# Token convolution stage: all eight chunks in one unrolled sequence, and expert loads split 24 and 40

## The chip, the cores and the metric

The kernel runs on one core of one Trainium2 chip. The metric is the device time of one execution in microseconds (us). The engines named below are TensorE (PE; its weight loads are listed apart, as PEld), VectorE (DVE), ScalarE (ACT), GpSimd (POOL) and SyncE (SP); the last issues most of the DMAs, POOL the gathers.

## What is computed

A small language-model tower over 16 x 256 tokens of 64 features, nine stages one after the other. The change is in the first stage, and it moves work across the border to the second.

```python
def _L0_tok_ref(x, emb, W, b):           # first stage
    offsets = jnp.arange(-(KSIZE // 2), KSIZE // 2 + 1)        # KSIZE = 9
    idx = jnp.clip(x[..., None] + offsets, 0, INP_SIZE - 1)
    gathered = emb[idx]                                        # 9 neighbouring rows of the table
    out = jnp.einsum('btkh,ohk->bto', gathered, W) + b
    return out
...
h = _L0_tok_ref(...)
h = h + _L0_attn_ref(_layernorm(h), ...)  # second stage, linear attention
h = h + _L0_ffn_ref(_layernorm(h), ...)   # third stage: each run of 64 tokens has one of 16 experts
...
```

## The kernel before, in words

Tokens are cut into `CHUNKS` = 8 chunks of 512; a chunk is four groups of 128 tokens. `W` = 4 chunks are in work at a time, each with a PSUM tensor `PS[w]` of its own, two banks wide; `ITERS` = 2 rounds of four chunks cover all. `H` holds the tower's running result.

In `token_convolution` each chunk goes through this chain. POOL issues four indirect DMAs (L226), each of which fetches for 128 tokens the nine neighbouring table rows, 2304 bytes in one piece. The buffer `win` has six slots, so chunk 6 has to wait until PE has read chunk 0 (`windows_read`), chunk 7 until chunk 1. PE transposes the first half of the windows into `PS[w]` (eight transposes, L246, r = 0; called r0 in the prediction); DVE and ACT copy one bank each to `winT` (L302, L283); PE transposes the second half (r1), and they copy again (L305, L286). PE transposes the tails, the ninth row (L256, L257), and ACT copies them (L289). PE convolves: eight matmuls (L264), each shown twice, and one for the tails (L267). ACT copies the result (L292), PE transposes it back (L274), and DVE adds the bias into `H` (L310).

The order on PE is by steps over a whole round: r0 of all four chunks, r1 of all four, tails of all four, convolution of all four, turning back of all four; then the second round, which first waits until all four chunks of the first are in `H`. PE's program is written out; ACT's is a hardware loop of two rounds. In the last round DVE also prepares the layer norm of the second stage (`prepare_next`): statistics and, after POOL's power, the normalised values of chunks 0 to 3. A block ends when every engine has reached its end.

SP issues the weights, and then in `Experts.load` (L513 to L515) one load of 129 KB for each run of 64 tokens, 64 in all: it reads the expert's number from `route`, and issues the DMA from a hardware loop. 32 loads (chunks 0 to 3) stand in the first stage's block and 32 in that of `linear_attention`. They are needed by the third stage, `routed_ffn`, whose POOL program begins with a wait for all of them.

Of the kernel before, what the change touches and what calls it, by code (L numbers as in the profile page):

```python
# [17 lines left out]
ALU = mybir.AluOpType  # L18
# [81 lines left out]

class NormBuffers:


# [64 lines left out]
def prepare_next(nc, v, H, C, stats, apply):  # L170

    N, x_of = C.next_norm, lambda w: groups(chunk_of(H, 0, w))
    N.prepared = True
    if stats:
        norm_stats(nc, v, N.S, x_of, N, 0)
    if apply and N.centre_only:
        norm_centre(nc, v, N.S, x_of, N, N.xc)
    elif apply:
        norm_apply(nc, v, N.S, x_of, N, N.xc, N.xn, 0)
# [11 lines left out]
def token_convolution(nc, H, PS, C, dram):  # L191
    with ExitStack() as ctx:
        S = semaphores(nc, "tok",
                        "ids windows_read winT_low winT_high winT_ps0 winT_ps1 winT2_low winT2_high "
                        "tailT yT_ps yT y_ps h_new")
        sb = lambda name, shape, dt=F32: ctx.enter_context(nc.sbuf_tensor(name, shape, dt))
        ids = sb("tok_ids", [P, CHUNKS * G4], I32)
        slots = W + 2
        slot = lambda it, w: it * W + w if w < slots - W else w - it * (slots - W)
        win = sb("tok_windows", [P, slots, G4, KS * D])  # L200
        winT = sb("tok_windowsT", [P, W, KC, G4 * P])
        tailT = sb("tok_tailsT", [P, W, U * P])
        yT = sb("tok_yT", [P, W, U * P])
        block = ctx.enter_context(nc.Block())
        gathered = [nc.alloc_semaphore(f"tok_gathered{c}") for c in range(CHUNKS)]
        w_main = C["tok_w"][:, 0:KC * D].rearrange("p (k f) -> p k f", f=D)
        w_tail = C["tok_w"][:, KC * D:]

        @block.sync
        def _(sp):  # L210
            sp.dma_start(ids[:], dram["ids"]).then_inc(S["ids"], 16)
            C.experts.load_route(sp)
            C.load(sp, "early")
            C.load(sp, "gate")
            C.experts.load(sp, range(CHUNKS // 2))

        @block.gpsimd
        def _(pool):
            pool.wait_ge(S["ids"], 16)
            for it in range(ITERS):  # L220
                for w in range(W):
                    if it * W + w >= slots:
                        pool.wait_ge(S["windows_read"], it * W + w - slots + 1)
                    for g in range(G4):
                        at = (it * W + w) * G4 + g
                        nc.gpsimd.indirect_dma_start(  # L226
                            win[:, (it * W + w) % slots, g, :], None, dram["emb"],
                            bass.IndirectOffsetOnAxis(ap=ids[:, at:at + 1], axis=0)).then_inc(gathered[it * W + w], 16)
            prepare_next_rstd(nc, pool, C)

        @block.tensor
        def _(pe):
            ident = C["ident"]
            pe.wait_ge(C.sem("base"), C.count("base"))
            for it in range(ITERS):
                for r in range(KC // 2):
                    for w in range(W):
                        if r == 0:
                            pe.wait_ge(gathered[it * W + w], 16 * G4)
                        else:  # L240
                            pe.wait_ge(S["winT_low"], it * W + w + 1)
                            pe.wait_ge(S["winT_high"], it * W + w + 1)
                        for k in range(2):
                            for g in range(G4):
                                at = (2 * r + k) * P
                                ins = nc.tensor.transpose(PS[w][:, k, g * P:(g + 1) * P], win[:, slot(it, w), g, at:at + P],  # L246
                                                          ident)
                        ins.then_inc(S["winT_ps0"] if r == 0 else S["winT_ps1"], 1)
                for w in range(W):
                    pe.wait_ge(C.sem("base"), C.count("base"))  # L250
                    pe.wait_ge(S["winT2_low"], it * W + w + 1)
                    pe.wait_ge(S["winT2_high"], it * W + w + 1)
                    for u in range(U):

                        tails = PS[w][:, 0, u * P:(u + 1) * P]
                        nc.tensor.transpose(tails, win[:, slot(it, w), 2 * u + 1, KC * P - D:], ident)  # L256
                        ins = nc.tensor.transpose(tails[0:D], win[:, slot(it, w), 2 * u, KC * P:], ident)  # L257
                    ins.then_inc(S["windows_read"], 1)
                for w in range(W):
                    odd_even = lambda ap: ap.rearrange("p (u h q) -> p h u q", u=U, h=2)  # L260
                    y = [PS[w][h * D:(h + 1) * D, 1, 0:U * P] for h in range(2)]
                    for k in range(KC):
                        for h in range(2):
                            nc.tensor.matmul(y[h], w_main[:, k, :], odd_even(winT[:, w, k, :])[:, h], start=(k == 0),  # L264
                                             stop=False)
                    pe.wait_ge(S["tailT"], it * W + w + 1)
                    nc.tensor.matmul(PS[w][:, 1, 0:U * P], w_tail, tailT[:, w], start=False, stop=True)\  # L267
                        .then_inc(S["yT_ps"], 1)
                for w in range(W):
                    pe.wait_ge(C.sem("base"), C.count("base"))  # L270
                    pe.wait_ge(S["yT"], it * W + w + 1)
                    for u in range(U):
                        at = slice(u * P, (u + 1) * P)
                        ins = nc.tensor.transpose(PS[w][:, 0, at], yT[:, w, at], ident)  # L274
                    ins.then_inc(S["y_ps"], 1)
                pe.wait_ge(S["h_new"], it * W + W)

        @block.scalar
        def _(act):
            with act.Fori(0, ITERS) as it:  # L280
                for w in range(W):
                    act.wait_ge(S["winT_ps0"], it * W + w + 1)
                    nc.scalar.copy(winT[:, w, 1, :], PS[w][:, 1, :]).then_inc(S["winT_high"], 1)  # L283
                for w in range(W):
                    act.wait_ge(S["winT_ps1"], it * W + w + 1)
                    nc.scalar.copy(winT[:, w, 3, :], PS[w][:, 1, :]).then_inc(S["winT2_high"], 1)  # L286
                for w in range(W):
                    act.wait_ge(S["windows_read"], it * W + w + 1)
                    nc.scalar.copy(tailT[:, w], PS[w][:, 0, 0:U * P]).then_inc(S["tailT"], 1)  # L289
                for w in range(W):  # L290
                    act.wait_ge(S["yT_ps"], it * W + w + 1)
                    nc.scalar.copy(yT[:, w, :], PS[w][:, 1, 0:U * P]).then_inc(S["yT"], 1)  # L292
                act.wait_ge(S["y_ps"], it * W + W)

        @block.vector
        def _(v):
            v.wait_ge(C.sem("base"), C.count("base"))

            def one_round(it, last):
                for w in range(W):  # L300
                    v.wait_ge(S["winT_ps0"], it * W + w + 1)
                    nc.vector.tensor_copy(winT[:, w, 0, :], PS[w][:, 0, :]).then_inc(S["winT_low"], 1)  # L302
                for w in range(W):
                    v.wait_ge(S["winT_ps1"], it * W + w + 1)
                    nc.vector.tensor_copy(winT[:, w, 2, :], PS[w][:, 0, :]).then_inc(S["winT2_low"], 1)  # L305
                if last:
                    prepare_next(nc, v, H, C, True, True)
                for w in range(W):
                    v.wait_ge(S["y_ps"], it * W + w + 1)
                    nc.vector.tensor_tensor(groups(chunk_of(H, it, w)), groups(PS[w][:, 0, 0:CW]),  # L310
                                            bcast(C["tok_b"], 1, G4), ALU.add).then_inc(S["h_new"], 1)
                v.wait_ge(S["h_new"], it * W + W)

            with v.Fori(0, ITERS - 1) as it:
                one_round(it, False)
            one_round(ITERS - 1, True)

# [3 lines left out]
def linear_attention(nc, H, PS, C, dram):  # L323
    with ExitStack() as ctx:
# [16 lines left out]

        @block.sync
        def _(sp):
            C.experts.load(sp, range(CHUNKS // 2, CHUNKS))

        @block.gpsimd
        def _(pool):
# [2226 lines left out]
```

## Time and profile before

| | us |
|---|---|
| median of three runs (lowest to highest) | 947.04 (946.51 to 947.96) |
| the profiled execution | 946.42 |
| its span, first to last instruction | 944.6 |
| first stage: last addition into `H` ends | 80.5 |
| second stage: its block ends | about 148.6 |
| mean granted TensorE clock | 0.865 |

All times of a row are counted from the first instruction of the span. The page's own summary:

```profile
span 944.6 us, 13089 instructions
PE 703.9 (75%) x4437; PEld 447.7 (47%) x4437; DVE 560.0 (59%) x1472; ACT 337.7 (36%) x612; POOL 200.0 (21%) x170
DMA  8552221000000100000000000005001000000001
```

A digit of the last line is the mean busy share, in tenths, of the core's 16 DMA engines in one fortieth of the span (23.6 us). A row of the timeline gives start, duration, engine, line, operation and what it writes and reads, then in brackets how long the engine was idle before and who released it. The engine name SPq is SP's own instruction stream.

### The profile page before, as it was taken

Reading aid. Unit: us, or ns where it says so; the run is one execution under the profiler, and the core shown is the slowest. Engines: PE = TensorE matmul, PEld = TensorE weight load, DVE = VectorE, ACT = ScalarE, POOL = GpSimd, SP = SyncE. Lnnn points to the kernel's source line nnn. Section 1 sums busy time; section 2 is a strip of 40 time slices with the busy share of each in tenths; the row PEclk is TensorE's granted clock in tenths of the full one; section 3 lists DMA queues with packets and bytes.
Section 4 is the critical chain, followed back from the end, with each engine's and each line's share of the span. In section 5 each row is a group of like instructions: output and inputs, shape, how many; then the busy total and the mean of one; then the engine's idle time right before and its main releaser. Section 6 shows DMA issues by size and latency. Waiting matters only on the chain. (4 is left out here: it accounts for less than half of the span.)

```text
span 944.6 us, 13089 instructions
## 1 busy us (share of the span) xinstructions
PE 703.9 (75%) x4437; PEld 447.7 (47%) x4437; DVE 560.0 (59%) x1472; ACT 337.7 (36%) x612; POOL 200.0 (21%) x170
## 2 busy tenths in 40 slices
PE   2587667978882699987489856877785978999674
PEld 1465555647661323224365435543221645887363
DVE  0144883444547557756685278645556899444597
ACT  1132112425451345434123312412333958333253
POOL 6421110130201010113520133110204557000320
PEclk9799787988996599997679977995978989899887
DMA  8552221000000100000000000005001000000001
GB/s 281 175 154 74 79 63 59 2 1 1 1 1 0 60 1 1 1 29 1 1 1 1 1 1 1 1 22 231 1 0 32 1 0 0 1 1 2 1 14 32
DMA packets 17708, 31.38 MB, mean 33 GB/s; under 512 B 6226, under 2 KB 14450, under 8 KB 16882
## 3 DMA queue, kind: packets, MB, share of 16 engines
q1 hardware_dynamic: 15090, 21.18, 7.1%
q0 software_dynamic: 2560, 9.44, 3.2%
q8 instruction: 35, 0.57, 0.3%
q14 instruction: 23, 0.19, 0.1%
HBM read 29.54 MB, written 1.05 MB: 32 GB/s over the span
## 5 line engine op out<-in xcount | busy, mean ns | idle before, releaser
L150 POOL TENSOR_TENSOR norm_rstd<-norm_var,minus_half 128x16 f32<-128x16 f32 x16 | 47.5, 2967 | 398.3 <-DVE norm_var L144 398.3
L1184 ACT ACTIVATE m_g<-PS,w_slot 128x512 f32<-128x512 f32 x96 | 60.8, 686 | 70.6 <-PE PS L1237 64.3
L1137 DVE TENSOR_TENSOR m_gw<-m_g,PS 128x512 f32<-128x512 f32 x96 | 61.4, 683 | 39.2 <-PE PS L1245 26.7
L1237 PE MATMUL PS<-m_xT,w_slot 64*128 64x512 f32 x192 | 70.9, 696 | 7.0 <-ACT m_g L1184 6.8
L1261 PE MATMUL PS<-m_gw,w_slot 128*64 128x512 f32 x192 | 56.4, 657 | 0.0
L1392 POOL TENSOR_TENSOR win_rms<-win_ms,win_minus_half 128x24 f32<-128x24 f32 x8 | 33.3, 4164 | 89.3 <-DVE win_ms L1438 89.3
L246 PE MATMUL PS<-w_base,tok_windows 128*128 128x128 f32 x128 | 21.1, 337 | 29.4 <-DMA tok_windows<-in_emb,tok_ids 21.2
L1531 DVE TENSOR_TENSOR win_out<-PS,w_slot 128x512 f32<-128x512 f32 x32 | 20.6, 686 | 33.0 <-PE PS L1702 33.0
L1245 PE MATMUL PS<-m_gT,m_sel 48*128 48x512 bf16 x96 | 24.3, 423 | 15.8 <-DVE m_gw L1137 10.0
L1968 ACT COPY rat_xf<-PS 64x512 f32 x32 | 33.7, 1053 | 5.4 <-PE PS L2024 5.2
L1700 PE MATMUL PS<-win_big,win_v 128*128 128x512 f32 x64 | 32.2, 627 | 4.4 <-ACT win_big L1604 4.2
L226 POOL DMA_INDIRECT tok_windows<-in_emb,tok_ids x32 | 30.6, 957 | 21.9 <-PE PS L257 9.5
L2044 PE MATMUL PS<-w_slot,rat_ht 128*128 128x256 f32 x128 | 34.7, 396 | 0.0
L132 DVE BATCH_NORM_STATS2 norm_halves<-H 128x6 f32<-128x64 f32 x256 | 33.9, 216 | 0.9 <-PEq L2550 0.9
L1594 ACT ACTIVATE win_terms<-win_terms 128x768 f32<-128x768 f32 x8 | 6.8, 845 | 75.9 <-DVE win_terms L1494 75.9
L246 PEld LDWEIGHTS PS<-w_base,tok_windows 128*128 128x128 f32 x128 | 19.0, 177 | 31.0 <-issue 13.1
L1237 PEld LDWEIGHTS PS<-m_xT,w_slot 64*128 64x128 f32 x192 | 24.2, 217 | 18.2 <-ACT m_g L1184 14.9
L2024 PE MATMUL PS<-w_slot 128*128 128x512 f32 x64 | 31.6, 618 | 0.0
L1657 PE MATMUL PS<-w_base,win_big 128*128 128x128 f32 x64 | 12.9, 368 | 22.8 <-DVE win_big L1469 22.8
L1245 PEld LDWEIGHTS PS<-m_gT,m_sel 48*128 48x128 bf16 x96 | 5.5, 94 | 50.1 <-DVE m_gw L1137 30.3
L1914 DVE COPY rat_hf<-PS 128x512 f32 x16 | 16.6, 1040 | 20.7 <-PE PS L2044 20.7
L302 DVE COPY tok_windowsT<-PS 128x512 f32<-128x512 f32 x8 | 5.4, 690 | 38.4 <-issue 19.9
(331 smaller groups left out, 1715.2 us busy)
## 6 DMA issues: line engine op xcount, KB each, us to landing
rff_routed<-in_routed SPq DMA_DIRECT2D x64, 129.0 KB, 2.0
rat_hf<-in_rat_den SPq DMA_DIRECT2D x1, 2048.0 KB, 7.7
rat_hf<-in_rat_num SPq DMA_DIRECT2D x1, 2048.0 KB, 12.2
w_slot<-in_w_rat SPq DMA_DIRECT2D x1, 1716.5 KB, 15.8
w_slot<-in_w_win SPq DMA_DIRECT2D x1, 1379.5 KB, 5.9
w_slot<-in_w_m SPq DMA_DIRECT2D x1, 1329.0 KB, 6.0
w_slot<-in_w_early SPq DMA_DIRECT2D x1, 1156.0 KB
out<-H SPq DMA_DIRECT2D x8, 128.0 KB, 2.2
```

The costliest lines, as they stand in the source:

```text
L132: ins = nc.vector.bn_stats(N.st[:, w * G4 + g, :], x_of(w)[:, g, :])
L150: nc.gpsimd.tensor_tensor(N.rstd[:], N.var[:], C.minus_half[:], ALU.pow).then_inc(S["norm_rstd"], 1)
L246: ins = nc.tensor.transpose(PS[w][:, k, g * P:(g + 1) * P], win[:, slot(it, w), g, at:at + P], ident)
L1137: nc.vector.tensor_tensor(gw[:, i % 2, half, :], g[:, i % 2, half, :], gate_bank[half], ALU.mult)\
L1184: nc.scalar.activation(g[:, i % 2, half, :], hid_bank[(n - 1) % 3], ACT.Gelu, bias=b1[:, s:s + 1])\
L1237: nc.tensor.matmul(hid_bank[n % 3], w1[lane(half), s, :], pair_of(xT, pair)[lane(half)], start=True, stop=True).then_inc(S["hid_ps"], 1)
L1261: ins = nc.tensor.matmul(y[half], w2[:, s, :], gw[:, i % 2, half, :], start=False, stop=(s == SL - 1))
L1392: nc.gpsimd.tensor_tensor(rms[:, w].rearrange("p u j h -> p (u j h)"), ms[:, w].rearrange("p u j h -> p (u j h)"), minus_half[:], ALU.pow)\
L1700: ins = nc.tensor.matmul(PS[w][:, u, :], v[:, w, u, half, :], probT[w][:, half * U + u, :], start=True, stop=(u == 0))
L1968: ins = nc.scalar.copy(dst, banks[4 + s % 4][rows, :].rearrange("p (t x l) -> p t x l", t=2, x=2))
L2024: ins = nc.tensor.matmul(banks[4 + s % 4], xd[:, w, 2 * u + half].rearrange("p a f -> p (a f)"), dft[:, u, :], start=(u == 0), stop=(u == ...
L2044: ins = nc.tensor.matmul(bank[:, 2 * LT:], part_of[c], odd[:, c, :], start=(c == 0), stop=(c == 1))
```

## The change

`ladder` is new. It puts each chunk's stages at fixed steps: stage k of chunk c comes at step `spacing * c + k`, with spacing 2, so a chunk enters every two steps and a chunk's own stages (r0, r1, tails, convolution, turning back) follow in consecutive steps. PE, ACT and DVE all follow it, written out for all eight chunks; the hardware loops of ACT and DVE in this stage are gone. PE's waits for the end of a round are replaced by a wait for the chunk that used the same `PS[w]` last. DVE's norm statistics are placed at step 11 and the application at step 14. The buffers keep their sizes, and no operation of a chunk is added or removed. In a step the order on PE is: turn back, convolve, tails, r1, r0. SP's 64 expert loads are cut after chunk 2: 24 in the first block, 40 in the second.

```diff
+def ladder(stages, depth, spacing, then=None):
+
+    for n in range(spacing * (CHUNKS - 1) + depth):
+        for k, stage in stages:
+            if n >= k and (n - k) % spacing == 0 and (n - k) // spacing < CHUNKS:
+                stage((n - k) // spacing)
+        if then:
+            then(n)
...
+        spacing, depth = 2, 5
...
-            C.experts.load(sp, range(CHUNKS // 2))
+            C.experts.load(sp, range(3))
...
-            for it in range(ITERS):
-                for r in range(KC // 2):
-                    for w in range(W):
-                        if r == 0:
-                            pe.wait_ge(gathered[it * W + w], 16 * G4)
...
-                pe.wait_ge(S["h_new"], it * W + W)
+            def turn_windows(c, r):
+                w = c % W
+                if r == 0:
+                    pe.wait_ge(gathered[c], 16 * G4)
+                    if c >= W:
+                        pe.wait_ge(S["h_new"], c - W + 1)
+                else:
+                    pe.wait_ge(S["winT_low"], c + 1)
+                    pe.wait_ge(S["winT_high"], c + 1)
...
+            def turn_tails(c):
+                w = c % W
+                pe.wait_ge(S["winT2_low"], c + 1)
...
+            def convolve(c):
+                w = c % W
+                pe.wait_ge(S["winT2_high"], c + 1)
...
+            ladder([(4, turn_y), (3, convolve), (2, turn_tails), (1, lambda c: turn_windows(c, 1)),
+                    (0, lambda c: turn_windows(c, 0))], depth, spacing)
...
-            with act.Fori(0, ITERS) as it:
...
+            ladder([(3, copy_y), (2, copy_tails), (1, lambda c: copy_windows(c, 1)), (0, lambda c: copy_windows(c, 0))],
+                   depth, spacing)
...
+            def then(n):
+                if n == spacing * 3 + 5:
+                    v.wait_ge(S["h_new"], W)
+                    prepare_next(nc, v, H, C, True, False)
+                if n == spacing * 3 + 8:
+                    prepare_next(nc, v, H, C, False, True)
+
+            ladder([(4, add_bias), (1, lambda c: copy_windows(c, 1)), (0, lambda c: copy_windows(c, 0))], depth, spacing,
+                   then)
+            v.wait_ge(S["h_new"], CHUNKS)
...
-            C.experts.load(sp, range(CHUNKS // 2, CHUNKS))
+            C.experts.load(sp, range(3, CHUNKS))
```

## Rows read from the trace of the kernel before

**Rows 1.** Busy time by stretch; columns are named in the first line.

```profile
core 0: us, PE busy (x) PEld busy (x) DVE busy (x) ACT busy (x) POOL busy (x), PEclk, DMA share, GB/s
...
20.50:38.00 17.50, 6.30 (x32) 5.67 (x32) 0.69 (x1) 0.59 (x1) 10.44 (x11) 0.88 0.75 231
38.00:43.60 5.60, 4.77 (x23) 4.65 (x24) 3.87 (x6) 3.43 (x7) 0.00 (x0) 0.50 0.26 71
...
47.40:55.50 8.10, 5.90 (x37) 3.04 (x36) 0.00 (x0) 0.58 (x2) 4.74 (x5) 1.00 0.90 283
...
59.80:81.00 21.20, 19.94 (x160) 15.01 (x160) 12.68 (x44) 8.50 (x17) 3.06 (x1) 1.00 0.31 82
```

**Rows 2.** Timeline, first gather burst: PE's transposes and DVE's copies that follow them.

```profile
13.10 1.94 PE L246 MATMUL PS<-w_base,tok_windows 128*128 128x128 f32 x8 [13.10 <-DMA tok_windows<-in_emb,tok_ids]
...
15.07 0.69 DVE L302 COPY tok_windowsT<-PS 128x512 f32<-128x512 f32 x1 [15.07 <-issue]
...
17.73 1.97 PE L246 MATMUL PS<-w_base,tok_windows 128*128 128x128 f32 x8 [2.69 <-DMA tok_windows<-in_emb,tok_ids]
...
20.54 0.69 DVE L302 COPY tok_windowsT<-PS 128x512 f32<-128x512 f32 x1 [4.78 <-issue]
...
22.05 1.97 PE L246 MATMUL PS<-w_base,tok_windows 128*128 128x128 f32 x8 [2.36 <-DMA tok_windows<-in_emb,tok_ids]
...
27.12 4.33 PE L246 MATMUL PS<-w_base,tok_windows 128*128 128x128 f32 x24 [3.10 <-DMA tok_windows<-in_emb,tok_ids]
...
38.08 1.29 DVE L302 COPY tok_windowsT<-PS 128x512 f32<-128x512 f32 x2 [16.85 <-remote]
...
38.83 3.67 PE L246 MATMUL PS<-w_base,tok_windows 128*128 128x128 f32 x16 [7.38 <-DVE tok_windowsT L302]
```

**Rows 3.** Timeline, second gather burst: PE's last convolution matmul and ACT's copy behind it.

```profile
46.79 0.70 PE L267 MATMUL PS<-tok_tailsT,w_base 128*128 128x256 f32 x2
...
49.30 0.70 PE L267 MATMUL PS<-tok_tailsT,w_base 128*128 128x256 f32 x2
...
50.88 0.37 ACT L292 COPY tok_yT<-PS 128x256 f32<-128x256 f32 x1 [5.49 <-PE PS L267]
...
55.30 0.74 ACT L292 COPY tok_yT<-PS 128x256 f32<-128x256 f32 x2 [4.04 <-remote]
```

**Rows 4.** Line L226, POOL's gathers, in 4 to 35 us and in 43 to 54 us.

```profile
L226 POOL DMA_INDIRECT tok_windows<-in_emb,tok_ids x24: 945/949/1197, 4.1 to 33.2; - x24
...
L226 POOL DMA_INDIRECT tok_windows<-in_emb,tok_ids x8: 947/949/949, 43.6 to 52.4; - x8
```

**Rows 5.** SP's expert loads (L515) by stretch, SP's timeline, its waits.

```profile
L515 SPq DMA_DIRECT2D rff_routed<-in_routed x9: 13/351/716, 4.8 to 35.2; - x9
...
22.61 13.32 SPq L515 DMA_DIRECT2D rff_routed<-in_routed  x2
...
L515 SPq DMA_DIRECT2D rff_routed<-in_routed x12: 347/349/351, 60.8 to 78.2; - x12
...
SPq L192 <- PEq L192: 2.2, 1, 2.2
```

**Rows 6.** Timeline of the second round, when all windows have landed.

```profile
59.86 7.21 PE L246 MATMUL PS<-w_base,tok_windows 128*128 128x128 f32 x64 [0.77 <-DVE H L310]
...
60.99 0.59 ACT L283 COPY tok_windowsT<-PS 128x512 f32<-128x512 f32 x1 [0.28 <-PE PS L246]
...
68.74 1.95 PE L264 MATMUL PS<-tok_windowsT,w_base 128*64 128x256 f32 x16
70.62 0.70 PE L267 MATMUL PS<-tok_tailsT,w_base 128*128 128x256 f32 x2
71.25 1.95 PE L264 MATMUL PS<-tok_windowsT,w_base 128*64 128x256 f32 x16
...
78.68 1.13 PE L274 MATMUL PS<-w_base,tok_yT 128*128 128x128 f32 x8
79.09 1.42 DVE L310 TENSOR_TENSOR H<-PS,w_base 128x256 f32<-128x256 f32 x4 [3.59 <-PE PS L274]
```

**Rows 7.** SP in the second stage: its loads, and its wait at the block's end.

```profile
L515 SPq DMA_DIRECT2D rff_routed<-in_routed x32: 342/350/356, 82.6 to 133.8; - x32
...
SPq L324 <- PEq L324: 14.3, 1, 14.3
```

More of the change, by code:

```diff
@@ L198, in token_convolution @@
         slots = W + 2
-        slot = lambda it, w: it * W + w if w < slots - W else w - it * (slots - W)
+        spacing, depth = 2, 5
         win = sb("tok_windows", [P, slots, G4, KS * D])
@@ L219, in _ @@
             pool.wait_ge(S["ids"], 16)
-            for it in range(ITERS):
-                for w in range(W):
[L222 to L228, printed above, removed]
+            for c in range(CHUNKS):
+                if c >= slots:
+                    pool.wait_ge(S["windows_read"], c - slots + 1)
+                for g in range(G4):
+                    at = c * G4 + g
+                    nc.gpsimd.indirect_dma_start(
+                        win[:, c % slots, g, :], None, dram["emb"],
+                        bass.IndirectOffsetOnAxis(ap=ids[:, at:at + 1], axis=0)).then_inc(gathered[c], 16)
             prepare_next_rstd(nc, pool, C)
@@ L234, in _ @@
             pe.wait_ge(C.sem("base"), C.count("base"))
-            for it in range(ITERS):
-                for r in range(KC // 2):
-                    for w in range(W):
-                        if r == 0:
-                            pe.wait_ge(gathered[it * W + w], 16 * G4)
[L240 to L275, printed above, removed]
-                pe.wait_ge(S["h_new"], it * W + W)
@@ new lines, in turn_windows @@
+            def turn_windows(c, r):
[7 more added lines that the diff above has]
+                    pe.wait_ge(S["winT_high"], c + 1)
+                for k in range(2):
+                    for g in range(G4):
+                        at = (2 * r + k) * P
+                        ins = nc.tensor.transpose(PS[w][:, k, g * P:(g + 1) * P], win[:, c % slots, g, at:at + P], ident)
+                ins.then_inc(S["winT_ps0"] if r == 0 else S["winT_ps1"], 1)
@@ new lines, in turn_tails @@
+            def turn_tails(c):
+                w = c % W
+                pe.wait_ge(S["winT2_low"], c + 1)
+                for u in range(U):
+                    tails = PS[w][:, 0, u * P:(u + 1) * P]
+                    nc.tensor.transpose(tails, win[:, c % slots, 2 * u + 1, KC * P - D:], ident)
+                    ins = nc.tensor.transpose(tails[0:D], win[:, c % slots, 2 * u, KC * P:], ident)
+                ins.then_inc(S["windows_read"], 1)
+            def convolve(c):
+                w = c % W
+                pe.wait_ge(S["winT2_high"], c + 1)
+                odd_even = lambda ap: ap.rearrange("p (u h q) -> p h u q", u=U, h=2)
+                y = [PS[w][h * D:(h + 1) * D, 1, 0:U * P] for h in range(2)]
+                for k in range(KC):
+                    for h in range(2):
+                        nc.tensor.matmul(y[h], w_main[:, k, :], odd_even(winT[:, w, k, :])[:, h], start=(k == 0),
+                                         stop=False)
+                pe.wait_ge(S["tailT"], c + 1)
+                nc.tensor.matmul(PS[w][:, 1, 0:U * P], w_tail, tailT[:, w], start=False, stop=True).then_inc(S["yT_ps"], 1)
@@ L278, in _, with turn_y @@
+            def turn_y(c):
+                w = c % W
+                pe.wait_ge(S["yT"], c + 1)
+                for u in range(U):
+                    at = slice(u * P, (u + 1) * P)
+                    ins = nc.tensor.transpose(PS[w][:, 0, at], yT[:, w, at], ident)
+                ins.then_inc(S["y_ps"], 1)
+            ladder([(4, turn_y), (3, convolve), (2, turn_tails), (1, lambda c: turn_windows(c, 1)),
+                    (0, lambda c: turn_windows(c, 0))], depth, spacing)
         @block.scalar
@@ L279, in _, with copy_windows @@
         def _(act):
-            with act.Fori(0, ITERS) as it:
[L281 to L293, printed above, removed]
+            def copy_windows(c, r):
+                w = c % W
+                act.wait_ge(S["winT_ps1"] if r else S["winT_ps0"], c + 1)
+                nc.scalar.copy(winT[:, w, 2 * r + 1, :], PS[w][:, 1, :]).then_inc(S["winT2_high"] if r else S["winT_high"], 1)
@@ new lines, in copy_tails, with copy_y @@
+            def copy_tails(c):
+                act.wait_ge(S["windows_read"], c + 1)
+                nc.scalar.copy(tailT[:, c % W], PS[c % W][:, 0, 0:U * P]).then_inc(S["tailT"], 1)
+            def copy_y(c):
+                act.wait_ge(S["yT_ps"], c + 1)
+                nc.scalar.copy(yT[:, c % W, :], PS[c % W][:, 1, 0:U * P]).then_inc(S["yT"], 1)
+            ladder([(3, copy_y), (2, copy_tails), (1, lambda c: copy_windows(c, 1)), (0, lambda c: copy_windows(c, 0))],
+                   depth, spacing)
@@ L297, in _, with copy_windows, add_bias @@
             v.wait_ge(C.sem("base"), C.count("base"))
[L299 to L316, printed above, removed]
+            def copy_windows(c, r):
+                w = c % W
+                v.wait_ge(S["winT_ps1"] if r else S["winT_ps0"], c + 1)
+                nc.vector.tensor_copy(winT[:, w, 2 * r, :], PS[w][:, 0, :]).then_inc(S["winT2_low"] if r else S["winT_low"], 1)
+            def add_bias(c):
+                v.wait_ge(S["y_ps"], c + 1)
+                nc.vector.tensor_tensor(groups(H[:, c * CW:(c + 1) * CW]), groups(PS[c % W][:, 0, 0:CW]),
+                                        bcast(C["tok_b"], 1, G4), ALU.add).then_inc(S["h_new"], 1)
+            def then(n):
[7 more added lines that the diff above has]
+            v.wait_ge(S["h_new"], CHUNKS)
 def linear_attention(nc, H, PS, C, dram):
```

## The prediction

> **What bounds the kernel now.** Only the first stage changes its order, so I read the table of stretches over it first, then the timeline of PE with the copies that answer it, then the gathers, and SP last. The stage has three candidates for its end: the arrival of the windows, PE's own work, and SP's expert loads.
>
> The windows come in two bursts. 24 gathers are issued from 4.1 to 33.2 us, one every 1.25 us; then POOL waits for a free slot, and eight more go from 43.6 to 52.4 [rows 4]. PE's work can be read where nothing holds it, in the second round: 64 transposes in 7.2 us, so 0.9 for a block of eight; the tails fill the gap up to 68.7, 0.45 a chunk; a convolution takes 2.5 from start to start; turning back 1.1 for four, 0.28 a chunk [rows 6]. That is 5.0 us a chunk, 40 us for eight, at the full clock. PE is 94% busy there (19.94 of 21.2) [rows 1].
>
> The first round is quite different. In 20.5 to 38 PE is busy for 6.3 of 17.5 us, and DVE and ACT do one copy each [rows 1]. PE finishes chunk 0's block at 15.04 and the copy starts at 15.07. Chunk 1's ends at 19.70, its copy starts 0.8 us late, at 20.54. Chunk 2's ends at 24.02, and its copy starts at 38.08, 14 us late, though DVE had nothing else to do [rows 2]. In the second burst the same thing: a convolution that ends at 47.5 is answered at 50.88, one that ends at 50.0 at 55.30 [rows 3]. So while gathers run, PE's signals arrive late, and the delay ends about when the windows of the burst have landed. I call this the freeze. It is the main fact for this change, since the new order has more such handshakes inside the bursts. The name "remote" of the releaser says that the profile does not show what released it.
>
> SP suffers as well: nine loads in the first 35 us, with over 12 us between the eighth (22.6) and the ninth. Undisturbed it needs (78.2 - 60.8) / 11 = 1.58 us a load. It was done only 2.2 us before the block's end [rows 5]; with 32 loads in the block the end could come hardly 2 us earlier, whatever PE does. So PE and SP are both nearly on the path now.
>
> **The change part by part.** First the windows. POOL's wait for chunk 6 hangs on the tails of chunk 0, now PE's third block instead of its ninth. If the signal comes through, gathers run without a pause: 4.1 + 32 x 1.25 = 44.2, and with the 3.0 us that chunk 3 took from its last issue (24.1) to PE's start (27.12) the last windows are there at 47.2 instead of about 56 [rows 2, 4].
>
> PE if handshakes pass. r0 of chunk 0 ends at 15.0, the copy at 15.8; r1 in the slow form (1.97 for eight) ends 17.8, copy 18.6, tails 0.9 to 19.5, r0 of chunk 1 to 21.4, convolution 0 at double price to 26.4 [rows 2, 6]. The double price is the nearest row: eight transposes take 1.94 to 1.97 there against 0.9 later, and 38 to 43.6 shows the same with a granted clock of 0.50, the 1.2 GHz level, after PE had idled [rows 1, 2]. With PE now nearly always busy I take the full level afterwards. r1 of chunk 1, turning back chunk 0, tails 1 and r0 of chunk 2 end at 29.4. From here each chunk costs 5.0 plus one wait that the old order hid: the tails of a chunk come right behind its r1, and need DVE's copy of 0.69 and some 0.1 for two signals, of which the turning back of the chunk before fills 0.28; 0.5 left. Five more chunks at 5.5 bring r0 of chunk 7 to 56.9, ten us behind its windows, so arrival is no longer the bound. Then convolution 6 2.5, r1 0.9, copy 0.8, tails 0.45, convolution 7 2.7, copy 0.45, back 0.3, addition 0.4: 65.4, against 80.5 now.
>
> DVE's statistics and normalisation move to steps 11 and 14. They take about 3 us each between PE's signals; behind them on DVE stand the copies of chunks 6 and 7. Between the copies of r0 and the demand of r1 lies a convolution of 2.5, so I price this at nothing, with 1 us as its bound if that cover fails. POOL's power stands behind the last gather, which is issued by 44 to 50, long before step 11. The end-of-round waits that vanish are worth about 1 us (the gap before 59.86), contained in the sum.
>
> The loops. ACT's first copy after its loop edge waits 0.28 us for PE, no more than any other [rows 6]; unrolling is worth 0 here. By the Trainium skill ("Runtime: NRT & Kernel Launch", Instruction fetch mechanics) a taken branch outside the fetched window costs a fetch from memory and full unrolling avoids it; no wait of this stage's rows is at the branch, and by that rule the sum would gain at most the 0.28.
>
> SP. 24 loads in place of 32. From 60.8 on the pace is 1.58, so the 24th is issued at 60.8 + 3 x 1.58 = 65.5 under today's pause in the gathers, and SP is done 0.6 later, 66.1. If gathers run on to 47, the slow pace lasts longer: ninth at 35.2, the tenth one slow interval (12.6) later at 47.8, then 14 x 1.58 = 22.1, so 69.9 and done at 70.5 [rows 5]. These are the two ends; I take 70.5, since unbroken gathers are what the PE sum assumed. SP then ends the block, 5 us behind PE.
>
> The second block gets 40 loads. 31 intervals took 51.2 us, 1.65 each (a stretch of them is slower); SP waited 14.3 at the end. Eight more take 13.2, so 1.1 us of slack remain [rows 7]. Priced at 0, bound 1 us; the third stage's wait for the last landing gets no later than its start.
>
> The sum: the first block ends at 70.5 instead of 81.0 (78.8 + 2.2), a gain of about 10.4. The profiled execution gives 946.4 - 10.4 = 936.0; the median of the runs lies 0.6 above the profiled one, so 936.6, rounded to **937**.
>
> **The rivals.** *Freeze (slower).* Chunk 1's r0 ends at 21.4, where signals are between 0.8 us late (19.7) and 14 us late (24.0). If it is caught, nothing follows in the new order: r1 of chunk 1 needs its copy, and PE has only convolution 0 to do, where the old order still had r0 of chunks 2 and 3 and two r1 blocks. Chunk 0's tails (19.5) would just come through, chunk 6's gathers run on to 39.2, and the freeze to their landing at 42. PE has then done 5.6 of its 40 us; left are 34.3, six waits of 0.5, 2.5 for the slow clock after idling (5 us at half speed), 3 us for a second freeze by chunk 7's gathers (the old one left PE about that idle before 55.5), 1 for the end: 85.8, that is 5.3 later than now, **952**. It decides if a signal given between 20 and 24 us waits for the landing. For it: six of six handshakes deep in a burst did. Against it: the delays grow with the work PE had queued behind the gathers (40 transposes ran unanswered from 22 to 31.5 us; two convolutions in the second burst), and the new order queues little: the handshakes with a short queue before them, at 15 and 20 us, passed with the DMA engines as busy.
>
> *SP is not held.* By the Trainium skill ("DMA: Bandwidth & Descriptors", Queues, rings and completion order) each DMA engine alternates between the queues that have work, packet by packet. That rule alone would let expert loads pass beside gathers; the trace's interval of 12.6 us speaks against it. As a mechanism in rows: 24 loads at 1.58 end by 43, and PE sets the end at 65.4, a gain of 15: **932**.
>
> *Half frozen.* Some handshakes pass late, PE loses 10 to 14 of the 15 us, and the time stays at 945 to 949.
>
> *The second block overruns or the norm falls on the path.* 1 to 5 us given back: 938 to 942.
>
> **How the numbers follow.** Forecast 0.36 (about 934 to 939), SP not held 0.14, second block or norm 0.06, half frozen 0.10, freeze 0.34. Within 0.2% (945.1 to 948.9, about what a measurement of this kernel can tell from no change) lies the half-frozen case: same 0.10, faster 0.36 + 0.14 + 0.06 = 0.56, slower 0.34. Both signs hold much, so the range goes from 931 to 953; the forecast's own is 933 to 940.
>
> **What would show it.** Right: gathers issued without a pause from 4 to 44 us; copies within 1 us of PE's blocks all through; PE above 85% busy from 27 to 62; SP's block wait near zero with its last load at 66 to 70; the second stage's length unchanged at 67.6. The freeze would show as DVE and ACT idle for over 10 us after a PE block, releaser "remote", and as a first block that ends after 81. Wrong in any case if SP's pace outside bursts is not 1.58, or PE drops to 0.50 in the middle of the ladder.

## The result and the profile after

The changed kernel takes 958.69 us (957.58 to 960.18, four runs) against 946.77 (945.58 to 947.96, four runs): a ratio of 1.0129, interval 1.0111 to 1.0147. The forecast of 937 lies on the wrong side, and above all the time lies beyond the range. The profiled execution has 957.58 us, its span is 955.8, 11.2 more than before. Block by block, read from the ends of the blocks on SP (the same barriers in both traces), this is where it went:

| block | before | after | difference |
|---|---|---|---|
| first stage ends at | 81.0 | 88.3 | +7.3 |
| linear attention | 67.6 | 68.0 | +0.4 |
| routed_ffn | 56.6 | 57.1 | +0.4 |
| batchnorm_attention | 101.1 | 98.5 | -2.7 |
| gelu_moe_128 and window_attention | 327.7 | 327.9 | +0.3 |
| gelu_moe_64 | 90.4 | 93.1 | +2.7 |
| rational_convolution | 158.2 | 158.5 | +0.4 |
| depth_ffn, the last | 61.3 | 63.7 | +2.4 |

(Differences are taken before rounding.) Two thirds of the loss are in the changed stage, the rest in stages whose code is the same, but for the eight loads that moved into the second. First the stretches of the changed kernel, which answer [rows 1]:

```profile
core 0: us, PE busy (x) PEld busy (x) DVE busy (x) ACT busy (x) POOL busy (x), PEclk, DMA share, GB/s
...
20.50:38.00 17.50, 6.09 (x30) 4.04 (x30) 0.40 (x1) 0.67 (x2) 13.23 (x15) 0.83 0.83 252
38.00:47.00 9.00, 2.58 (x11) 2.18 (x12) 1.62 (x3) 1.45 (x3) 0.93 (x1) 0.50 0.38 116
47.00:60.00 13.00, 11.36 (x80) 8.41 (x79) 2.81 (x6) 3.56 (x8) 3.78 (x4) 0.92 0.57 167
```

PE is busy for 6.1 us of 17.5 in the gathers, and then 2.6 of 9.0; the old order had work for the second stretch as well (4.8 of 5.6 in 38 to 43.6). The timeline, which answers [rows 2]:

```profile
15.57 1.97 PE L257 MATMUL PS<-w_base,tok_windows 128*128 128x128 f32 x8 [0.86 <-ACT tok_windowsT L298]
...
20.21 0.69 DVE L318 COPY tok_windowsT<-PS 128x512 f32<-128x512 f32 x1 [4.69 <-remote]
...
21.87 1.92 PE L257 MATMUL PS<-w_base,tok_windows 128*128 128x128 f32 x8
23.71 2.64 PE L277 MATMUL PS<-tok_windowsT,w_base 128*64 128x256 f32 x16
...
27.20 0.37 ACT L302 COPY tok_tailsT<-PS 128x256 f32<-128x256 f32 x1 [6.41 <-remote]
...
43.32 0.69 DVE L318 COPY tok_windowsT<-PS 128x512 f32<-128x512 f32 x1 [22.41 <-remote]
43.80 0.38 ACT L306 COPY tok_yT<-PS 128x256 f32<-128x256 f32 x1
44.06 1.97 PE L257 MATMUL PS<-w_base,tok_windows 128*128 128x128 f32 x8 [15.74 <-DVE tok_windowsT L318]
```

r1 of chunk 0 ends at 17.5 and is answered 2.7 us late; the tails end at 22.1 (the fourth starts at 21.65 and takes 0.42) and are answered at 27.2; r0 of chunk 1 ends at 23.8 and its copy starts at 43.32, 19.5 us late. All that PE could do meanwhile was convolution 0, answered at 43.80. Then PE stands for 15.74 us. This is the rival "freeze", except that the rival had let the tails come through in time. The gathers answer [rows 4], SP's waits [rows 5]:

```profile
L235 POOL DMA_INDIRECT tok_windows<-in_emb,tok_ids x28: 942/946/1197, 4.0 to 38.0; - x28
...
48.20 0.94 POOL L235 DMA_INDIRECT tok_windows<-in_emb,tok_ids  x1 [9.27 <-PE PS L267]
```

```profile
SPq L202 <- PEq L202: 21.1, 1, 21.1
SPq L342 <- PEq L342: 2.0, 1, 2.0
```

Chunk 6's gathers did run on, chunk 7's waited for PE until 48.2. SP was done 21 us before the block's end, so it held nothing here; in the second block, with 40 loads, it was done 2.0 us before the end. The free-running part of the ladder shows its price per chunk:

```profile
58.61 1.04 PE L257 MATMUL PS<-w_base,tok_windows 128*128 128x128 f32 x8
...
64.31 1.04 PE L257 MATMUL PS<-w_base,tok_windows 128*128 128x128 f32 x8
...
66.13 0.33 PE L266 MATMUL PS<-w_base,tok_windows 128*128 128x128 f32 x1 [0.57 <-DVE tok_windowsT L318]
...
87.45 0.42 DVE L322 TENSOR_TENSOR H<-PS,w_base 128x256 f32<-128x256 f32 x1 [3.82 <-PE PS L287]
```

5.70 us a chunk (64.31 - 58.61), with the wait of 0.57 before the tails, against the 5.0 of [rows 6].

### The profile page after: what moved, and what is told of

Same layout as the page of the kernel before. It is cut to its first block and busy times, and to the rows that moved or that the text cites. A ratio compares the mean times of both kernels' runs of the same rounds, so it can differ in the third digit from the quotient of the medians.

```text
span 955.8 us, 13059 instructions
## 1 busy us (share of the span) xinstructions
PE 706.2 (74%) x4437; PEld 447.2 (47%) x4437; DVE 560.0 (59%) x1472; ACT 336.3 (35%) x611; POOL 198.8 (21%) x170
## 5 line engine op out<-in xcount | busy, mean ns | idle before, releaser
L1155 DVE TENSOR_TENSOR m_gw<-m_g,PS 128x512 f32<-128x512 f32 x96 | 61.4, 683 | 41.8 <-PE PS L1263 28.1
L1255 PE MATMUL PS<-m_xT,w_slot 64*128 64x512 f32 x192 | 70.5, 694 | 6.9 <-ACT m_g L1202 6.8
L318 DVE COPY tok_windowsT<-PS 128x512 f32<-128x512 f32 x16 | 11.1, 691 | 64.6 <-remote 27.1
L257 PE MATMUL PS<-w_base,tok_windows 128*128 128x128 f32 x128 | 20.9, 318 | 29.4 <-DVE tok_windowsT L318 15.7
```

Of the source, the lines that this page charges most:

```text
L1155: nc.vector.tensor_tensor(gw[:, i % 2, half, :], g[:, i % 2, half, :], gate_bank[half], ALU.mult)\
L1255: nc.tensor.matmul(hid_bank[n % 3], w1[lane(half), s, :], pair_of(xT, pair)[lane(half)], start=True, stop=True).then_inc(S["hid_ps"], 1)
```

## The experiments

Theory F: the loss comes from the freeze, that is from PE's blocks being answered late while gathers run, which the new order meets with too little work queued. Rivals: the split 24 and 40; the ladder as such; the bytes of the gathers; SP's loads beside them. Each group of runs was on another chip, which turned out to be the main finding. All runs in one table; "beside" is the unchanged kernel on the same chip, "block 1" the end of the first block in the profile:

| run | chip | us | beside | block 1 |
|---|---|---|---|---|
| the pair above: before / after | not named | 946.77 / 958.69 | | 81.0 / 88.3 |
| split_only | 3 | 936.61 | 937.11 | 69.5 |
| ladder_32 | 3 | 934.42 | 937.11 | 66.7 |
| narrow_ladder | 3 | 931.73 | 937.11 | 63.3 |
| narrow_rounds | 3 | 933.86 | 937.11 | 68.0 |
| after_again | 5 | 934.86 | 935.92 | 65.5 |
| before_again | 5 | 933.88 | 935.92 | 68.7 |
| spacing1 | 5 | 931.76 | 935.92 | 64.1 |
| paced | 5 | 935.59 | 935.92 | 66.0 |
| after_third | 15 | 936.13 | 938.79 | 66.1 |
| loads_late | 15 | 953.91 | 938.79 | 84.6 |
| narrow_third | 15 | 934.56 | 938.79 | 64.5 |
| spacing1_timed | 15 | 933.21 | 938.79 | 64.1 |
| narrow_fourth | 2 | 932.77 | 939.05 | 63.8 |
| spacing1_fourth | 2 | 931.55 | 939.05 | 63.9 |
| narrow_fifth | 9 | 933.01 | 938.89 | 64.1 |
| after_sixth | 7 | 935.91 | 934.09 | 66.5 |
| narrow_sixth | 7 | 933.79 | 934.09 | 64.3 |

split_only, after_again, ladder_32 and spacing1_timed have seven to ten runs; the others one. On chips 3, 5 and 15 the unchanged kernel ran 42 times, between 933.2 and 939.8.

### The two parts of the change alone

split_only is the kernel before with this edit:

```diff
-            C.experts.load(sp, range(CHUNKS // 2))
+            C.experts.load(sp, range(3))
...
-            C.experts.load(sp, range(CHUNKS // 2, CHUNKS))
+            C.experts.load(sp, range(3, CHUNKS))
```

> The kernel before, with only the expert loads cut 24 and 40. Theory (the freeze of PE's signals in the gather bursts, met by the new order, makes the whole loss): the first stage still ends at 80.5 to 81, since PE ends it, and the second grows by 0 to 1 us: ratio 1.000 to 1.001. Rival (the split costs, because 40 loads overrun the second stage): the second stage grows by 2 us or more, ratio 1.002 or above.

Measured: ratio 0.9986, interval 0.9971 to 1.0002. The split costs nothing that can be measured here. The block end of 81 was missed: it came at 69.5, with PE's copies all in time. (In the pair above, where the second block was done 2.0 us after SP, it cost nothing that shows either: that block is 0.4 longer.)

ladder_32 is the changed kernel with the loads cut 32 and 32 again:

```diff
-            C.experts.load(sp, range(3))
+            C.experts.load(sp, range(CHUNKS // 2))
...
-            C.experts.load(sp, range(3, CHUNKS))
+            C.experts.load(sp, range(CHUNKS // 2, CHUNKS))
```

> The changed kernel with 32 and 32 loads as before. Theory of the freeze: SP waited 21 us at the end of the changed first block, and 8 loads take 12.6 us, so the block still ends at 88; the ratio to the kernel before stays 1.012 to 1.013, at most 0.5 us better than the changed kernel. Rival (split costs): the ratio falls to 1.010 or lower.

Measured: ratio 0.9961, interval 0.9939 to 0.9983. The theory's expectation failed, and the rival's "1.010 or lower" is met by the number alone, since split_only shows no cost of the split: the ladder, 1.3% slower in the pair above, is 0.4% faster here, and its block ends 2.8 us before that of split_only on the same chip. SP had 12.7 us left in it. So neither the split nor the ladder makes the loss by itself; something else differs between the chips, or between the times of the measurements.

### The same two kernels on other chips

> The changed kernel, unaltered, on whatever chip it gets. Theory F (a freeze of PE's signals, which only some chips or states show, decides the sign): where the profile shows no copy later than 2 us behind PE's block, the first block ends at 66 to 68 and the ratio to the kernel before is 0.995 to 0.998; where it shows the freeze (copies over 10 us late between 20 and 43), the block ends at 86 to 90 and the ratio is 1.011 to 1.015. Rival (40 loads in the second stage cost more than the first stage gains): the ratio is 1.00 or more without any freeze.

> The kernel before, unaltered, for its profile beside the one of the changed kernel on the same chip. Theory F: without a freeze the first block ends at 69 to 71 and the time is 934 to 939; with it the block ends at 80 to 82 and the time is 945 to 948. The loads' pace tells the same: 1.5 to 1.6 us from the start without, one interval of over 10 us with the freeze.

Measured for the changed kernel, ten runs on chip 5: 934.86, ratio 0.9984, interval 0.9966 to 1.0002. The profiles of both on chip 5 show no freeze. The expectations were just missed (blocks at 65.5 and 68.7 instead of 66 to 68 and 69 to 71, the ratio a little above 0.998), and the interval does not quite exclude 1.00, the number of the rival that the second stage takes the gain; but that stage is only 1.0 us longer (68.6 against 67.6). The unchanged kernel there, to be laid beside [rows 1] and [rows 2]:

```profile
20.50:38.00 17.50, 12.13 (x82) 10.69 (x82) 4.22 (x7) 4.91 (x10) 12.96 (x14) 1.00 0.95 316
```

```profile
22.76 1.97 PE L246 MATMUL PS<-w_base,tok_windows 128*128 128x128 f32 x8 [2.92 <-DMA tok_windows<-in_emb,tok_ids]
...
24.77 0.69 DVE L302 COPY tok_windowsT<-PS 128x512 f32<-128x512 f32 x1 [4.20 <-PE PS L246]
27.84 6.29 PE L246 MATMUL PS<-w_base,tok_windows 128*128 128x128 f32 x40 [3.11 <-DMA tok_windows<-in_emb,tok_ids]
...
29.84 0.69 DVE L302 COPY tok_windowsT<-PS 128x512 f32<-128x512 f32 x1 [4.38 <-PE PS L246]
```

Chunk 2's transposes end at 24.73 and are answered at 24.77, where [rows 2] has 14 us. The releaser has a name again (PE, not "remote"). PE does 12.1 us of work in the stretch instead of 6.3. The DMA engines are busier than on the first chip, 0.95 and 316 GB/s against 0.75 and 231: the freeze is no matter of full DMA engines. Part of the difference in rate is that POOL issues 14 gathers in the stretch instead of 11; the other part is SP's loads, which keep their pace inside the bursts:

```profile
L515 SPq DMA_DIRECT2D rff_routed<-in_routed x28: 347/350/372, 4.8 to 47.1; - x28
...
DMA to landing us min/median/max: 2.0/4.2/4.4
```

28 loads in 42.3 us, 1.57 each, where [rows 5] has nine in 30.4 us. They land after 4.2 us, against the 2.1 of loads issued when no gathers run, but that holds nothing up. By the Trainium skill ("DMA: Bandwidth & Descriptors", Queues, rings and completion order) the engines alternate between the queues packet by packet. On this chip the trace agrees: loads at full pace beside gathers, each landing 2 us later. The first chip's trace does not speak against it, as the prediction held, since there SP issued few loads in the burst, and their landings are not recorded.

What slowed there was SP's own instruction stream. The instruction that sets up each load takes, least, median and longest in ns, in the changed kernel on the first chip and on chip 5:

```profile
L533 SPq MOVE rff_routed<-in_routed x24: 2/29/701, 4.6 to 66.6; - x24
...
L533 SPq MOVE rff_routed<-in_routed x24: 29/29/29, 4.8 to 40.8; - x24
```

PE's stream slowed too. In the second burst of the kernel before, on the first chip, a convolution that waits for no other engine falls apart into single matmuls 0.7 us apart:

```profile
52.28 0.45 PE L264 MATMUL PS<-tok_windowsT,w_base 128*64 128x256 f32 x2 [0.63 <-issue]
...
53.71 0.38 PE L264 MATMUL PS<-tok_windowsT,w_base 128*64 128x256 f32 x1 [0.97 <-issue]
...
54.43 0.48 PE L267 MATMUL PS<-tok_tailsT,w_base 128*128 128x256 f32 x1 [0.34 <-issue]
```

So the freeze is not only PE's signals arriving late; whether a late copy comes from a late signal or from a slow stream of the engine that waits, the rows do not tell.

The changed kernel on chip 5:

```profile
20.50:38.00 17.50, 15.80 (x117) 11.30 (x116) 5.14 (x9) 5.38 (x11) 13.24 (x14) 1.00 0.96 319
```

```profile
19.48 1.91 PE L257 MATMUL PS<-w_base,tok_windows 128*128 128x128 f32 x8
...
21.43 0.69 DVE L318 COPY tok_windowsT<-PS 128x512 f32<-128x512 f32 x1 [2.91 <-PE PS L257]
...
64.62 0.42 DVE L322 TENSOR_TENSOR H<-PS,w_base 128x256 f32<-128x256 f32 x1 [3.82 <-PE PS L287]
```

The forecast's PE sum comes out here at both ends: r0 of chunk 1 ends at 21.4 (21.4 forecast) and is answered at 21.43; the last addition ends at 65.04 (65.4 forecast). Between them two errors cancel:

```profile
23.86 0.70 PE L280 MATMUL PS<-tok_tailsT,w_base 128*128 128x256 f32 x2
...
26.71 1.04 PE L257 MATMUL PS<-w_base,tok_windows 128*128 128x128 f32 x8
...
55.32 1.04 PE L257 MATMUL PS<-w_base,tok_windows 128*128 128x128 f32 x8
```

Convolution 0 ends at 24.56 instead of 26.4, because the double price was right for its first part only, and r0 of chunk 2 ends at 27.75 instead of 29.4. The next five chunks then take 28.6 us instead of 27.5. The rival "SP is not held" is this case: the 24th load is issued at 40.8.

> The changed kernel, unaltered, on a further chip. Theory F (some chips show the freeze of PE's signals, others not): either the first block ends at 65 to 67 and the kernel before takes 934 to 939 beside it, or the block ends at 86 to 90 and the kernel before takes 945 to 948. Rival (the freeze was an accident of single executions): any other pairing of the two.

> The changed kernel, unaltered, on a further chip. Without the freeze: first block ends at 65 to 67, the kernel before takes 933 to 940. With it: 86 to 90, and 945 to 948 for the kernel before.

Both came out as "without": blocks at 66.1 and 66.5, and the unchanged kernel at 933 to 940. So there are seven chips, one with the freeze in both kernels and, by their times, in all eight of its runs, and six without it in seventeen profiles (on chip 9 only narrow gathers were profiled, and the kernel before speaks by its time, 938.89). The pair's chip was not met again, so whether it is the chip or a state in which it was then can't be told. No experiment ran under the freeze: what is said of it rests on the two profiles of the pair.

### What in the gathers could make it

narrow_ladder and narrow_rounds gather 1024 bytes a token instead of 2304, and PE reads the first 256 elements twice, and the tails from there too:

```diff
-                        win[:, c % slots, g, :], None, dram["emb"],
+                        win[:, c % slots, g, 0:2 * P], None, dram["emb"],
...
-                        at = (2 * r + k) * P
+                        at = k * P
...
```

> The changed kernel with gathers of 1024 bytes a token instead of 2304; PE transposes the first 256 elements twice and takes the tails from there too, so the convolution is computed on wrong windows, with the same number and shape of instructions on every engine. Theory A (the freeze comes from the bytes that the gathers move, the DMA engines being 0.75 to 0.9 busy): the DMA share falls below 0.5, the copies follow PE within 1 us, PE sets the end of the first stage at 64 to 68 us. Theory B (it comes from the act of gathering, POOL's descriptors, at one gather every 1.25 us as before): the freeze stays, the first stage ends at 84 or later. Theory C (the ladder is slow by itself): as A without a freeze, yet the end at 75 or later.

> The kernel before with the same narrow gathers of 1024 bytes. Theory A: no freeze; the first round is done at about 49, the second at about 70, but SP's 32 loads then set the end if they take 1.58 us each from the start (they would end at 56, so no); first stage ends at 68 to 72, later than in the ladder with narrow gathers by 2 to 6 us, so the change would have paid without the freeze. Theory B: freeze as before, end at 80.

Measured: blocks end at 63.3 and 68.0, so without a freeze the ladder is worth 4.7 us of the block with these gathers. Neither number proves anything for theory A, since this chip has no freeze with full gathers either; and the DMA share stayed at 0.71 in 20.5 to 38, where A expected less than 0.5.

> The changed kernel with gathers of 1024 bytes a token (wrong windows, same instructions), on the same chip as after_third. With a freeze there: gone if it comes from the bytes moved (block ends at 63 to 66), still there if from the act of gathering (84 or later). Without a freeze: the block ends 2 to 3 us before the changed kernel's, since the first windows land earlier, as on the first of these chips.

> The changed kernel with gathers of 1024 bytes a token (wrong windows, same instructions), on a further chip. If the kernel before takes 945 to 948 beside it, the chip shows the freeze, and then: gone from this kernel (block ends at 61 to 65) if it comes from the bytes moved, still there (84 or later) if from the act of gathering. If the kernel before takes 933 to 940, the chip shows none, and this kernel's block ends at 61 to 65.

> As narrow_fourth, on a further chip: if the kernel before takes 945 to 948 beside it the chip shows the freeze, and the first block of this kernel ends at 61 to 65 if the bytes moved make it, at 84 or later if the act of gathering does. If the kernel before takes 933 to 940 there is none, and the block ends at 61 to 65.

> As narrow_fifth, beside after_sixth on the same chip: with a freeze there, 61 to 65 if the bytes moved make it, 84 or later if the act of gathering does; without, 61 to 65.

64.5, 63.8, 64.1 and 64.3, each beside a kernel before of 934 to 940: no freeze on any of these chips, and the question of bytes against gathering stays open. (narrow_third is 1.6 us before after_third, where 2 to 3 were expected.)

loads_late holds SP's loads back:

```diff
+            sp.wait_ge(gathered[CHUNKS - 1], 16 * G4)
             C.experts.load(sp, range(3))
```

> The changed kernel with SP's 24 loads held back until the last windows have landed; so the bursts hold gathers alone, and SP's instruction stream is silent in them. With a freeze: if SP's traffic takes part in it, the copies follow PE within 2 us and gathers run to 44; if not, copies late by over 10 us as in the changed kernel. Without a freeze: loads end at 48 + 24 x 1.58 = 86, SP sets the end of the block at 86 to 87, the copies are as before.

Measured: the block ends at 84.6 (86 to 87 expected), and SP's wait for the last windows was 43.4 us. PE's work in the bursts is the same with and without loads beside the gathers:

```profile
20.50:38.00 17.50, 15.80 (x123) 11.63 (x122) 5.14 (x9) 5.75 (x12) 13.24 (x14) 1.00 0.81 236
```

15.80 us, as in after_again, at 236 GB/s instead of 319. 24 loads took from 48.1 to 84.5. This shows how SP's term works: with the loads at the end of the line SP sets the end of the block, 18.5 us after that of after_third on the same chip, and the kernel takes 17.8 us more than there. The loads beside the gathers do cost a little: without them PE starts at 12.19 instead of 13.14, and its part of the block is done at 63.9 instead of 65.7. 0.81 and 236 GB/s is also nearly the traffic of the frozen stretch in [rows 1], here without delay: the traffic that the DMA engines show does not by itself make the freeze.

### Other orders

spacing1 has one edit:

```diff
-        spacing, depth = 2, 5
+        spacing, depth = 1, 5
```

> The changed kernel with a chunk entering at every step instead of every second. With a freeze, theory F says that PE now has r0 of the next chunk queued where it stood still, but still only one block ahead, so the first block ends at 83 to 88. Without a freeze two chunks' work covers the wait of 0.5 to 0.7 us a chunk, and the block ends 2 to 5 us earlier than the changed kernel's. Rival (the ladder's 5.7 us a chunk is PE's own work): no gain from the closer spacing.

> The changed kernel with a chunk entering at every step, timed. Without a freeze: the first block 2 to 3 us shorter than the changed kernel's, ratio to the kernel before 0.994 to 0.997 (the later stages may give or take 3 us by their clock). With a freeze: ratio 1.005 to 1.013, since r0 of one more chunk is all that PE can do ahead.

> The changed kernel with a chunk entering at every step, on the same further chip. With a freeze there: the first block ends at 83 to 88, since PE has one more r0 to do ahead and no more. Without: 64 to 65.

Measured, without a freeze: blocks end at 64.1, 64.1 and 63.9, 1.4 us before the changed kernel on chip 5 and 2.0 on chip 15; ten runs give 933.21 and a ratio of 0.9955, interval 0.9931 to 0.9980. This is the lowest ratio of the kernels that compute the whole reference, though the interval of ladder_32 overlaps it. spacing1 gained less in the block than the 2 to 5 us that were expected. PE's stretch in the profile of spacing1_timed, in the columns used above, shows where the gain comes from:

```profile
38.00:47.00 9.00, 9.00 (x76) 6.93 (x75) 3.43 (x6) 3.53 (x8) 4.74 (x5) 1.00 0.88 289
```

PE is busy all the time, against 8.44 of 9.00 in after_again on chip 5: the wait of 0.57 before the tails is covered by another chunk. The end of the block shows why so little of it arrives:

```profile
60.77 0.42 DVE L322 TENSOR_TENSOR H<-PS,w_base 128x256 f32<-128x256 f32 x1 [2.65 <-PE PS L287]
61.11 1.42 DVE L166 TENSOR_TENSOR norm_xc<-H,norm_mean 128x256 f32<-128x256 f32 x4
62.44 1.43 DVE L176 TENSOR_TENSOR norm_xn<-norm_xc,norm_rstd 128x256 f32<-128x256 f32 x4
```

The last addition ends at 61.2, 4.5 us before that of the changed kernel on the same chip (65.7), but the block ends at 64.1, because DVE applies the norm until 63.87. The application stands at step 11, and with spacing 1 that is the last step, behind the last addition. An earlier place for it was not tried. How spacing 1 would do on the chip with the freeze was not seen.

paced makes POOL wait, from chunk 2 on, for the first copy of the chunk two before:

```diff
+                if c >= 2:
+                    pool.wait_ge(S["winT_low"], c - 1)
```

> The changed kernel with POOL gathering chunk c only when chunk c - 2's first copy is done, which leaves gaps in the gather traffic. With a freeze: if it needs a long unbroken burst to build up, the signals come through in the gaps and the first block ends by 75; if it starts anew within a chunk's gathers, the block ends at 88 or later. Without a freeze: gathers of one chunk every 5.7 us at most, and the block ends within 1 us of the changed kernel's.

Measured on chip 5: block at 66.0, 0.5 us after the changed kernel's. Pauses in the gathers cost next to nothing there; against the freeze they could not be tried.

### The stages that did not change

Without a freeze the changed block gains 3.2 us (68.7 to 65.5 on chip 5), yet the time gains only 1. The last stage is the clearest case. In the four profiles of the old order (the pair's before, before_again, split_only, narrow_rounds) it takes 61.3 or 61.4 us, in the fifteen of the ladder 63.2 or 63.7, with the same code. Its stretch from some 3 to 13 us after its start, before_again first, after_again second:

```profile
874.00:884.00 10.00, 6.07 (x24) 4.78 (x25) 7.96 (x33) 3.34 (x7) 7.52 (x6) 0.66 0.00 1
```

```profile
873.00:883.00 10.00, 6.03 (x18) 4.52 (x19) 7.47 (x32) 2.28 (x6) 7.47 (x6) 0.51 0.00 1
```

The granted clock is 0.66 in one and 0.51 in the other, so PE is at the 1.2 GHz level for nearly all of it, and does 18 matmuls instead of 24 in the same busy time. In all four profiles of the old order the granted clock is 0.50 for 6.8 us there, in all fifteen of the ladder for 10.2. Other stages that differ between profiles are gelu_moe_64 (90.1 to 94.6 us over all profiles) and batchnorm_attention (98.4 to 101.1); there the times do not follow the order of the first stage. Why the ladder leads to the longer slow stretch at the end was not tested and stays open.

## Why the prediction was wrong

**The reading of the first round.** The table of stretches and the late copies were read rightly, though not that SP's and PE's own streams slow down too: the freeze was named, and the rival for it foretold PE standing with only convolution 0 to do, release by the landing of chunk 6 (42 expected, 43.3 measured), the late gathers of chunk 7, and an end at 85.8 (87.9 measured). The step that failed is the choice between it and the forecast, at 0.34 against 0.36. The argument "short queues pass" fell: the four instructions of the tails were answered 5.1 us late, one block of eight 19.5 us late.

**The baseline of the sum.** This is the deeper error. The forecast took the block's end from a trace with the freeze (81.0) and set against it an end worked out without one (70.5). No chip shows this pair. With the freeze it is 81.0 to 88.3, without it 68.7 to 65.5. A gain of 10.4 in the block was in neither world; the measured sizes are +7.3 and -3.2. The sum for PE without the freeze was good to 0.4 us (65.4 against 65.04), in part by luck: convolution 0 at double price to its end was 1.8 us too much, and 5.5 us a chunk 1.1 too little over five chunks.

**SP's term.** 70.5 rested on the slow pace lasting on to 47.8 while PE ran freely. The interval of 12.6 us was read as loads that the gathers' traffic holds; it is SP's own instruction stream. In the pair the 24th load was issued at 66.6, and SP waited 21.1 us at the end; without a freeze it waited 24.1. It held the end in neither. The two go together: where PE's signals are late SP is slow, and where they are in time SP has its 1.57 us.

**The ladder's price per chunk** was 5.5 and measured 5.70; the wait before the tails was priced at 0.5 and shows 0.57. The norm on DVE was priced at nothing, bound 1 us; it delays one of DVE's copies (75.04, where ACT's copy of the same block starts at 73.39), and PE loses 0.1 us by it. Both right in kind; with spacing 1 the same norm ends the block, 2.7 us behind the last addition. The second freeze, priced at 3 us, was 1.2 (a block that ends at 52.8 is answered at 53.99).

**The split.** Priced at 0, bound 1 us: the slack of 2.0 to 2.5 us remained, and split_only shows no loss. Right.

**The stages behind.** Not in the sum at all: +3.8 us in the pair. They explain most of why the frozen case ended at 958.7 and not at 952: 2.1 us from the block, 3.8 from the later stages. Without them the profiled execution would stand at 953.8, still just outside the range. The stages' own two levels of clock are as large as the effect of the change on six of the seven chips.

## What to carry to other kernels

Before a disturbance in the trace is taken into a sum, put it into both sides or into neither: a sum of "before with it" against "after without it" is a case that no chip will run. A wait that ends in a releaser without a name, much later than the work it waits for, and with several engines slow together, asks for a second chip before anything is built on it. An order that leaves an engine several blocks of independent work (the old rounds) loses less to late signals than one that hands over after each block (the ladder), and spacing 1 shows that even without late signals one more chunk in flight covers the hand-over of 0.57 us. When the spacing of such a sequence is changed, look at what else is placed by its steps: the norm at step 11 went from inside the sequence to its end, and kept 2.7 us of the gain.

## What was not expected of the hardware

The same kernel takes 946.8 us on one chip and 934 to 939 on six others, and 12.3 of the 12.5 us between the two profiles (81.0 against 68.7) arise in the first block, in the 50 us in which gathers run. In that time PE's blocks are answered up to 19.5 us late and SP needs up to 12.6 us for a load, while POOL's gathers keep their 1.25 us and the windows land in time. What it is stays open: the DMA engines' load is ruled out as its sufficient cause (0.95 busy without it), and so is the presence of gathers with their bytes by themselves (236 GB/s without it). An untested rival is that the recording of the trace itself takes part. For it: in the first 38 us the two disturbed traces hold 158 and 156 landings of DMAs on semaphores, although their 24 and 28 gathers and nine loads were issued, while the traces of the same two kernels on chip 5 hold 767 each; so records are missing just where the engines are slow, and this may also be why the releasers have no name. The eight runs of the first chip agree within 0.3% for each kernel, but that does not speak against it, since the record has a span and a granted clock for each of them, so none is known to have run unrecorded.

And the order of the first stage goes with the length of the last one, some 780 us later: 1.8 to 2.4 us more in all fifteen profiles of the ladder, at a lower clock granted to TensorE.
